# A residual convolution and expert-mix kernel: the last unit split only in its last group, ScalarE's matrices ahead of its load

## The reference

```python
# layer 0: grouped convolution (4 groups, 9 taps) plus a term per sample and channel
out = lax.conv_general_dilated(x, weight, (1,), [(4, 4)], ..., feature_group_count=4)
x = x + out + (c @ c_weight.T)[:, :, None] + bias[None, :, None]
# layer 1: eight experts mixed per sample; att comes from a small MLP and a softmax over cond_128
agg_w = einsum('bk,koi->boi', att, weight[..., 0])
x = x + einsum('boi,bih->boh', agg_w, x) + (att @ bias_k)[:, :, None]
```

## Time and profile before

| | |
|---|---|
| time, median of 3 runs | 252.69 us (251.22 to 255.4) |
| the profiled execution | 251.88 us, its span 250.1 us |
| TensorE busy | 238.8 us (96% of the span) |
| VectorE busy | 220.8 us (88%) |
| ScalarE busy | 128.5 us (51%) |
| DMA | 68.60 MB, 274 GB/s over the span |
| convolution matmuls of whole groups (L552) | 1488 records, 166.7 us |
| mix matmuls (L575) | 480 records, 59.4 us |
| transposes of `phases` (L418), columns (L444), `y_natural` (L453) | 71.8, 74.5, 66.7 us |

### The profile page before, as it was taken

How to read it: one execution, slowest core, us unless ns; L and a number is a source line. 1 busy time by engine, 2 the same in 40 slices (tenths; PEclk the granted TensorE clock), 3 DMA queues, 4 the chain that set the end, 5 groups by cost and what they waited for, 6 DMA issues and landing times.

```text
span 250.1 us, 5822 instructions
## 1 busy us (share of the span) xinstructions
PE 238.8 (96%) x2186; PEld 103.0 (41%) x2186; DVE 220.8 (88%) x115; ACT 128.5 (51%) x208; POOL 10.4 (4%) x36
## 2 busy tenths in 40 slices
PE   7899899999999999999999999999999999999962
PEld 5633234444343444444443444344443444444631
DVE  0256699999999999999999999999999999999672
ACT  2564106534719083745639181836547286273863
POOL 1323200000000000000000000000000000000000
PEclk9799999999999999999999999999999999999999
DMA  7999935999989999999999998999989895444466
GB/s 201 260 290 273 270 66 184 263 317 369 362 300 303 334 242 375 240 387 233 358 264 313 317 301 310 258 381 229 377 241 348 271 313 242 168 170 169 168 246 260
DMA packets 29771, 68.60 MB, mean 274 GB/s; under 512 B 3312, under 2 KB 5744, under 8 KB 29760
## 3 DMA queue, kind: packets, MB, share of 16 engines
q1 hardware_dynamic: 19824, 51.12, 61.7%
q10 hardware_dynamic: 9936, 17.34, 26.2%
HBM read 34.89 MB, written 33.55 MB: 274 GB/s over the span
## 4 chain that ended last, share of the span: by engine, by line
PE 83%; DVE 5%; DMA 4%; ACT 3%; ACTq 2%; issue 1%
PE yps L552 59%; PE zps L575 21%; DMA xin<-in_x 4%; DVE xph L418 2%; DVE ynat L453 2%; PE yps L591 1%; ACTq L330 1%; PE yps L634 1%; DVE ycol L444 1%; ACT mixv L320 1%; ACT zout L311 1%; DVE ynat L498 1%; PE zps L614 0%; PE yps L614 0%; PE zps L603 0%
## 5 line engine op out<-in xcount | busy, mean ns | idle before, releaser
L552 PE MATMUL yps<-xph,wraw 64*64 64x512 f32 x1488 | 166.7, 589 | 1.7 <-DVE ycol L444 1.1
L552 PEld LDWEIGHTS yps<-xph,wraw 64*64 64x64 f32 x1488 | 66.5, 132 | 95.1 <-issue 95.0
L311 ACT ACTIVATE zout<-zps,gamu 128x512 f32<-128x512 f32 x120 | 72.8, 689 | 29.8 <-PE zps L575 19.9
L444 DVE STREAM_TRANSPOSE ycol<-yps 128x1024 f32<-128x1024 f32 x62 | 74.5, 1227 | 7.3 <-PE yps L552 5.5
L320 ACT ACTIVATE mixv<-mixt 64x256 f32 (+1 forms) x64 | 42.3, 660 | 67.0 <-issue 65.8
L418 DVE STREAM_TRANSPOSE xph<-xin 128x4160 f32<-128x4160 f32 (+2 forms) x17 | 71.8, 4223 | 3.9 <-DMA xin<-in_x 3.9
L453 DVE STREAM_TRANSPOSE ynat<-ycol 128x4096 f32<-128x4096 f32 x15 | 66.7, 4445 | 1.1
L575 PE MATMUL zps<-ynat,mixv 64*64 64x512 f32 x480 | 59.4, 592 | 0.4 <-DVE ynat L453 0.2
L575 PEld LDWEIGHTS zps<-ynat,mixv 64*64 64x64 f32 x480 | 20.6, 132 | 31.6 <-issue 31.2
L250 POOL COPY gamu<-gam 128x4 f32 (+1 forms) x16 | 2.9, 188 | 197.9 <-ACT zout L311 193.2
L634 PE MATMUL yps<-zout 128*128 128x256 f32 x26 | 9.8, 538 | 1.3 <-POOL zout L252 1.3
(11 more groups left out here) (54 smaller groups left out, 30.2 us busy)
## 6 DMA issues: line engine op xcount, KB each, us to landing
out<-zout SPq DMA_DIRECT2D x60, 512.0 KB, 4.6
xin<-in_x ACTq DMA_DIRECT2D x60, 258.0 KB, 7.4
xin<-in_x SPq DMA_DIRECT2D x60, 258.0 KB, 7.1
out<-xin SPq DMA_DIRECT2D x2, 512.0 KB, 4.2
out<-xin SPq DMA_DIRECT2D x4, 256.0 KB, 2.8
xin<-in_x ACTq DMA_DIRECT2D x4, 132.0 KB, 5.3
xin<-in_x SPq DMA_DIRECT2D x4, 130.0 KB, 5.9
xin<-in_x SPq DMA_DIRECT2D x4, 128.0 KB, 7.5
```

What stands on the lines that cost most here:

```text
L311: nc.scalar.activation(zout[:, o].rearrange("p (i c j q) -> p c i j q", i=2, c=2, q=PH)[:, c], zps[:, at:at + BANK].rearrange("p (q i j) - ...
L444: nc.vector.transpose(ycol[:, :, :, :, :, g].rearrange("p i s j q c -> p (i s j) q c"), yps[:, 2 * BANK * (g % 2):2 * BANK * (g % 2) + 2 * ...
L552: last = nc.tensor.matmul(yps[C * c:C * c + C, at:at + BANK].rearrange("p (s f) -> p s f", s=S // 2), wsum[rows, b, g], xph[slot][rows, g, ...
```

## The change

In ScalarE's program `matrices` now stands ahead of `load`, in the loop and in the two units written out ahead of it. In the last unit, group 2 is convolved whole, as in all other units, and only group 3 by halves; `conv_last`, `last_columns` and `y_last` lose their group argument. On TensorE mixes 0 and 1 of unit 14 stand together ahead of group 2, the first half of group 3 comes ahead of mixes 2 and 3, the second half behind them and ahead of `mix_first(0)`. On VectorE the constant is no longer added to part of pair 0; ScalarE does both parts of pairs 0 and 2, and VectorE now does the second halves of both pair 1 and pair 3. The last stores go out in the order pair 0, pair 2, then the halves of pair 1 and those of pair 3.

```diff
--- before.py
+++ after.py
@@ -156,9 +156,9 @@
             return out.rearrange("(b s) c l -> b (s c) l", s=2)[bass.ds(PR * u + o, 1)].rearrange("b p l -> (b p) l")
-        def y_last(g):
-            return yps[:, 2 * BANK * (g % 2):2 * BANK * (g % 2) + 2 * BANK].rearrange(
+        def y_last(sh):
+            return yps[:, 2 * BANK * (1 - sh):2 * BANK * (1 - sh) + 2 * BANK].rearrange(
                 "p (i h f) -> p h i f", i=2, h=2)[:, 0]
         def z_first(o):
@@ -228,12 +228,10 @@
             for u in range(NU - 4, NU - 1):
                 for o in range(PR):
                     store(u, o)
-            sp.wait_ge(z_act, 1)
-            sp.wait_ge(z_dve, 1)
-            sp.dma_start(z_rows(NU - 1, 0), out_last(0)).then_inc(z_out[0], 16)
-            sp.wait_ge(z_act, 3)
-            sp.dma_start(z_rows(NU - 1, 2), out_last(2)).then_inc(z_out[2], 16)
-            for o, i, made, n in ((1, 0, z_act, 4), (3, 0, z_act, 5), (1, 1, z_dve, 2), (3, 1, z_act, 6)):
+            for o in (0, 2):
+                sp.wait_ge(z_act, o + 2)
+                sp.dma_start(z_rows(NU - 1, o), out_last(o)).then_inc(z_out[o], 16)
+            for o, i, made, n in ((1, 0, z_act, 5), (1, 1, z_dve, 1), (3, 0, z_act, 6), (3, 1, z_dve, 2)):
                 sp.wait_ge(made, n)
                 sp.dma_start(z_rows(NU - 1, o)[:, H * i:H * i + H], out_half(o, i)).then_inc(z_out[o], 16)
             for o in range(PR):
@@ -363,22 +361,22 @@
             nc.scalar.activation(gam[:], gps[:, 0:NP], ACT.Copy).then_inc(gam_made, 1)
             for o in range(PR):
                 evacuate(0, 0, o)
+                if o == 1:
+                    matrices(1, 1)
                 if o % 2 == 1:
                     load(3 + o // 2, 1 - o // 2)
-                if o == 1:
-                    matrices(1, 1)
             for o in range(PR):
                 evacuate(1, 1, o)
                 if o == 1:
+                    matrices(2, 0)
                     load(5, 1)
-                    matrices(2, 0)
             with act.Fori(3, NU // 2) as i:
                 for c in range(2):
                     for o in range(PR):
                         evacuate(2 * i + c - 4, c, o)
                         if o == 1:
+                            matrices(2 * i + c - 3, 1 - c)
                             load(2 * i + c, c)
-                            matrices(2 * i + c - 3, 1 - c)
             for u in range(NU - 4, NU - 1):
                 for o in range(PR):
                     evacuate(u, u % 2, o)
@@ -399,17 +397,13 @@
                     z_half(o, i).rearrange("p c (q j) -> p c j q", q=PH),
                     ACT.Identity, bias=gamu[1][:, o:o + 1]).then_inc(z_act, 1)
-            act.wait_ge(last_mixes, 1)
-            evacuate_first(0, 0)
-            act.wait_ge(last_mixes, 2)
-            evacuate_first(2, 0)
-            evacuate_first(2, 1)
-            act.wait_ge(last_mixes, 3)
-            evacuate_half(1, 0)
-            act.wait_ge(last_mixes, 4)
-            evacuate_half(3, 0)
-            act.wait_ge(last_mixes, 6)
-            evacuate_half(3, 1)
+            for o in (0, 2):
+                act.wait_ge(last_mixes, 1 + o // 2)
+                for c in range(2):
+                    evacuate_first(o, c)
+            for o in (1, 3):
+                act.wait_ge(last_mixes, 3 + o // 2)
+                evacuate_half(o, 0)
         @block.vector
         def _(dve):
@@ -485,42 +479,36 @@
                 for c in range(2):
                     step(2 * i - 1 + c, 1 - c)
-            def last_columns(sh, g):
-                dve.wait_ge(last_conv, 2 * sh + g - 1)
+            def last_columns(sh):
+                dve.wait_ge(last_conv, sh + 1)
                 for i in range(2):
                     nc.vector.transpose(
-                        ycol[:, i, 2 * sh:2 * sh + 2, :, :, g].rearrange("p s j q c -> p (s j) q c"),
-                        y_last(g)[:, i].rearrange("p (n j t) -> p n t j", j=16, t=2)).then_inc(last_cols, 1)
+                        ycol[:, i, 2 * sh:2 * sh + 2, :, :, G - 1].rearrange("p s j q c -> p (s j) q c"),
+                        y_last(sh)[:, i].rearrange("p (n j t) -> p n t j", j=16, t=2)).then_inc(last_cols, 1)
             def last_natural(sh):
-                dve.wait_ge(last_cols, 4 * sh + 4)
+                dve.wait_ge(last_cols, 2 * sh + 2)
                 for i in range(2):
                     nc.vector.transpose(
                         ynat[1][:, :, :, i, 2 * sh:2 * sh + 2].rearrange("p t q s (j l) -> p (s j) q t l", l=16),
                         ycol[:, i, 2 * sh:2 * sh + 2].rearrange("p s j q g c -> p (s j q g c)")).then_inc(last_nat, 1)
-            y_columns(NU - 1, 0)
-            y_columns(NU - 1, 1)
-            dve.wait_ge(ycol_made, 4 * NU - 2)
-            last_columns(0, 2)
-            last_columns(0, 3)
+            for g in range(G - 1):
+                y_columns(NU - 1, g)
+            dve.wait_ge(ycol_made, 4 * NU - 1)
+            last_columns(0)
             dve.wait_ge(mix_done, 4 * NU - 8)
             last_natural(0)
-            last_columns(1, 2)
+            last_columns(1)
+            last_natural(1)
             dve.wait_ge(gam_cut, NU)
-            dve.wait_ge(last_mixes, 1)
-            nc.vector.tensor_scalar(
-                out_last(0).rearrange("p (i c j q) -> p c i j q", i=2, c=2, q=PH)[:, 1],
-                z_first(0)[:, 1].rearrange("p (q i j) -> p i j q", q=PH, i=2),
-                gamu[1][:, 0:1], None, ALU.add).then_inc(z_dve, 1)
-            last_columns(1, 3)
-            last_natural(1)
-            dve.wait_ge(last_mixes, 5)
-            nc.vector.tensor_scalar(
-                out_half(1, 1).rearrange("p (c j q) -> p c j q", c=2, q=PH),
-                z_half(1, 1).rearrange("p c (q j) -> p c j q", q=PH),
-                gamu[1][:, 1:2], None, ALU.add).then_inc(z_dve, 1)
+            for n, o in enumerate((1, 3)):
+                dve.wait_ge(last_mixes, 5 + n)
+                nc.vector.tensor_scalar(
+                    out_half(o, 1).rearrange("p (c j q) -> p c j q", c=2, q=PH),
+                    z_half(o, 1).rearrange("p c (q j) -> p c j q", q=PH),
+                    gamu[1][:, o:o + 1], None, ALU.add).then_inc(z_dve, 1)
         @block.tensor
         def _(pe):
@@ -578,20 +566,18 @@
                             start=True, stop=True)
                 last.then_inc(mix_done, 1)
-            def conv_last(sh, g):
-                if sh == 0:
-                    pe.wait_ge(ycol_made, 4 * NU - 5 + g)
-                else:
-                    pe.wait_ge(last_cols, 2 * g - 2)
+            def conv_last(sh):
+                pe.wait_ge(ycol_made, 4 * NU - 2 + sh)
                 for b in range(NT):
                     for i in range(2):
                         rows = slice(C * i, C * i + C)
                         for c in range(2):
                             last = nc.tensor.matmul(
-                                y_last(g)[C * c:C * c + C, i].rearrange("p (s f) -> p s f", s=2),
-                                wsum[rows, b, g],
-                                xph[1][rows, g, 2 * sh:2 * sh + 2, NJ * c + b:NJ * c + b + NJ].rearrange("p s j t -> p s (j t)"),
+                                y_last(sh)[C * c:C * c + C, i].rearrange("p (s f) -> p s f", s=2),
+                                wsum[rows, b, G - 1],
+                                xph[1][rows, G - 1, 2 * sh:2 * sh + 2, NJ * c + b:NJ * c + b + NJ].rearrange("p s j t -> p s (j t)"),
                                 start=b == 0, stop=b == NT - 1)
                 last.then_inc(last_conv, 1)
@@ -699,33 +685,31 @@
             conv(NU - 1, 1, 0)
             conv(NU - 1, 1, 1)
             mix(NU - 2, 0, 0)
-            conv_last(0, 2)
             mix(NU - 2, 0, 1)
-            conv_last(0, 3)
+            conv(NU - 1, 1, 2)
+            conv_last(0)
             mix(NU - 2, 0, 2)
-            conv_last(1, 2)
             mix(NU - 2, 0, 3)
+            conv_last(1)
             pe.wait_ge(mixv_made, 4 * NU)
             pe.wait_ge(last_nat, 2)
             pe.wait_ge(z_made, 8 * NU - 10)
             mix_first(0)
-            conv_last(1, 3)
             pe.wait_ge(z_made, 8 * NU - 8)
             mix_first(2)
             pe.wait_ge(last_nat, 3)
-            pe.wait_ge(last_cols, 8)
+            pe.wait_ge(last_cols, 4)
             mix_half(1, 0)
             mix_half(3, 0)
             pe.wait_ge(last_nat, 4)
-            pe.wait_ge(z_act, 1)
-            pe.wait_ge(z_dve, 1)
+            pe.wait_ge(z_act, 2)
             mix_half(1, 1)
-            pe.wait_ge(z_act, 3)
+            pe.wait_ge(z_act, 4)
             mix_half(3, 1)
```

## The result

| | before | changed |
|---|---|---|
| time, median | 251.67 us (22 runs) | 249.62 us (22 runs) |
| ratio to before, 95% interval | | 0.9922 (0.9905 to 0.9939) |
| profiled execution, its span | 251.88, 250.1 us | 250.47, 248.7 us |

The change takes 0.78% off, 1.96 us (1.5 to 2.4) by the ratio. The forecast was 1.85 us and a median of 250.8; it stood on the 252.69 of the three runs shown then, so the two are compared by what the change takes off.

The account below looks back on a forecast made before the run. Bound by TensorE's stalls behind late ScalarE, and by stores at the end. Loop 1.45 plus tail 0.4 gives 1.85 us off, a median of 250.8 us; 249.2 to 252.9 holds about 0.85.

Parts of the forecast that it names:

- What bounds the kernel: Whole kernel: TensorE busy 96%; 1.45 us lost in the middle to late ScalarE, the end set by waits and stores.
- The loop's edit: Loop: matrices fit ScalarE's idle 2.65 us, evacuation of pairs 2 and 3 comes 2.7 us earlier; gain 1.45 us.
- held the pace: Loop: VectorE's turns, 13.62 us apart, fit a unit of 13.75 us with 0.13 us to spare.
- The slower rival: Loop: ScalarE's copies beside VectorE's `phases` slow it; at 10% a cost of 3.8 us, 254.6 us; chance 0.05.
- The last unit's edit: Last unit: reordering ends the engines' work 1.5 us earlier, but the stores leave a gain of 0.4 us.
- The walk through the engines: Last unit: start and end times worked out for TensorE, ScalarE and VectorE; last constant ends 244.95 instead of 246.10.
- the later `mix_first(0)`: Last unit, TensorE: `mix_first(0)` waits for VectorE instead of ScalarE and starts at 239.61 instead of 238.94.
- first store: Last unit: pair 0's store is issued at 242.15 instead of 241.00, 1.15 us later.
- stores decide the end: Tail: six stores of 2.10 MB at 414, then 383 GB/s set the last byte, 248.2 against 248.59.
- the term for the tail: Tail: gain of 0.4 us, bounds a loss of 0.4 and a gain of 1.5.
- the stores eat the tail: Tail: pair 0's later store leaves a gain of 0.2 to a loss of 0.4, 251.0 to 251.7 us; chance 0.20.
- The issue of pair 0's store: Tail: taken as 0.33 us; if again 1.11, flow starts 0.8 us later and the tail loses 0.4.

Follow-up runs that it names:

- e1: The kernel before with only the loop's order changed, ScalarE's matrices ahead of its load, last unit as before; 0.9937 of before.
- e7: The changed kernel with ScalarE's load in the loop moved behind all evacuations of its step; 0.9896 of before.
- e3: The changed kernel with its six last stores cut to a quarter of their columns, engines' work unchanged; 0.9858 of before.
- e9: e1 with 24 tiny matmuls added to TensorE's program ahead of unit 0's first mix; tail 18.94 us.
- e4: The kernel before with its six last stores cut to a quarter of their columns; 0.9948 of before.
- e6: The changed kernel with group 2 ahead of mix 1, mix 3 behind half 1 and the last unit's matrices made earlier; 0.9965 of before.
- e10: e6 with 24 tiny matmuls added to TensorE's program ahead of unit 0's first mix; tail 18.42 us.
- e12: The changed kernel with 24 tiny matmuls added to TensorE's program ahead of unit 0's first mix, as a control; tail 18.76 us.
- e8: The changed kernel unchanged, run again beside later variants for comparison; 0.9931 of before.

## Why the prediction was right

**What bounds the kernel.** Six stalls of 1.45 us in all, put down to ScalarE's evacuation: all six went by moving `matrices` alone (e1), 1.43 to 1.44 us.

**The loop's edit.** Forecast 1.45, measured 1.43. The matrices found the idle time, and the load was not even issued later: at 84.32 on the clock of before (85.09 less 0.77), where it had stood at 84.31. A later load would not have been missed either (e7), and VectorE held the pace. The slower rival, ScalarE's copies slowing `phases`, did not happen: no step of the chain is longer than 6.88 us.

**The last unit's edit.** The walk through the engines holds to 0.05 us at each station, the later `mix_first(0)` and the later first store included, and so does the claim that stores decide the end (e3).

**The step that was off** is the term for the tail, 0.4 us, measured 0.76. I read the last byte of before at 248.59, as if all 16 DMA engines ended together, and took the 1.5 us from there to the end as fixed. What is fixed is the 0.85 us behind the last data; the rest was one engine that worked on alone until 249.25. Of the last store of before, 15 shares had landed by 249.03 and the last by 249.61, 0.58 us later; between e1 and e9, where only the packet moved, the difference is 0.33. So 0.33 to 0.58 us of the tail of before was one engine held up by a packet that goes with TensorE's program, and the new order happens to have that packet in a stretch without stores. What the reordering itself gives in the tail is 18.94 - 18.75 = 0.19 us (e9 against the changed kernel), half of my 0.4. So the sum came out near, 1.85 against 1.96 (1.5 to 2.4) by the ratio and 2.19 by the two traces, but in the tail that was luck: a mis-sized 0.2 of the order, and 0.57 that I did not know of. Without the packet's move the two edits are worth 1.43 + 0.19 = 1.6 us. The rival "the stores eat the tail", a gain of 0.2 to a loss of 0.4, was nearer for the order alone.

The issue of pair 0's store, which took 1.11 us before, was a peculiarity of that execution: in e1 and e4, with the same last unit, it took 0.33.

## What to carry to other kernels

When an engine issues DMAs and computes, look at what stands behind the issues: independent work put into a wait that is long anyway cost nothing here, and it was the larger part of the gain. When a tail ends in stores, add up their bytes from the first issue on before counting what the engines gain; and when one store takes much longer from issue to landing than the next, look for a packet on an instruction queue before trusting a comparison of orders, since 24 tiny matmuls far ahead moved the end by up to 1.7 us here (e6 and e10). And read the end of the last transfer finely enough to see a single engine of the 16.

## What the hardware showed that I had not expected

- A packet of 16 KB on the queue `q8 instruction`, seven or eight times in a run, occupies one of the 16 DMA engines for 0.9 to 1.5 us. With stores of 512 KB in flight, each landing in 16 shares, one share then landed 2.0 us after the other 15 in e6 (up to 2.4 in e4), and one share of each later store was late too, in e6 until the end. That packet and share are on the same engine is inferred from the moves of e9 to e12; the trace does not name engines. Why the share is later than the packet is long (1.5 us in e6) stays open. The Trainium skill has the size (Advanced Engine Details and Errata, ISA Cache: code is cached in lines of 16 KB, 256 instructions). That such a packet holds up data is what these runs show.
- The packet does not come at a fixed count: 128 weight loads behind the one before in the changed kernel (132 in e8, the same kernel), 160 in the kernel before and 184 in e1, which has the same program on TensorE, 188 in e6; and 24 or 50 matmuls more moved it otherwise than by their own number. That its place depends on TensorE's program is shown; that it is TensorE's code is inferred from this, from the counts and from the pause during the loop. What sets its moment stays open.
- An issue on SyncE's queue took 0.33 us in most places of the tail and 0.63 to 0.82 us in the changed kernel's last three, when 1.0 to 1.3 MB of stores had been issued and had not landed; once in e6 it took 1.4 us. The amount alone does not decide it: in e12 one took 0.88 us behind a single late store. It cost nothing that shows at the end, since the DMA engines were full the whole time.
